# A graph-attention kernel: the adjacency in half-size loads with three buffers, the small buffers over the loaded keys, and an eighth block of each tile transposed by DMA

## The reference

```
h = max(layernorm(x), 0)                       # 8192 x 128
s = leaky_relu(h @ ks.T, slope 0.2)            # 8192 x 8192
s = where(adj > 0, s, -9e15)
attn = softmax(s, axis=1)
out = x + attn @ ks                            # 8192 x 128
```

## Time and profile before

| | |
|---|---|
| median of three runs | 1670.91 us |
| the profiled execution: its own time | 1674.09 us |
| its span, first to last instruction | 1672.3 us |
| mean granted TensorE clock | 0.996 |
| TensorE matmuls busy | 1629.2 us (97%) |
| VectorE busy | 1504.9 us (90%) |
| ScalarE busy | 1436.1 us (86%) |
| GpSimd busy | 1048.3 us (63%) |
| DMA, mean rate | 240 GB/s |
| SyncE's queue, time of its packets | 101.3% of 16 engines' span |

### The profile page before, as it was taken

The page is one execution under the profiler, slowest core; times in us unless marked ns, Lnnn a source line. Parts: engine busy times, 40 slices in busy tenths (PEclk is TensorE's granted clock), DMA queues, the critical chain, the costliest instruction groups (busy, mean ns, idle before and its releaser), DMA issues.

```text
span 1672.3 us, 38378 instructions
## 1 busy us (share of the span) xinstructions
PE 1629.2 (97%) x13698; PEld 1213.1 (73%) x13698; DVE 1504.9 (90%) x2656; ACT 1436.1 (86%) x2145; POOL 1048.3 (63%) x1096
## 2 busy tenths in 40 slices
PE   5699999999999999999999999999999999999999
PEld 3377777777777777777777777777777777777777
DVE  7999989999999999999998989989989998999896
ACT  6688888888888888888888888888888888888887
POOL 1466666666666765765766766666656666666665
PEclk9999999999999999999999999999999999999999
DMA  6699999999999999999999999999999999999996
GB/s 208 179 240 245 252 240 248 249 241 251 236 250 245 240 257 241 247 253 252 237 243 235 258 251 233 248 252 245 243 230 256 243 246 246 242 253 234 248 251 123
DMA packets 536892, 401.00 MB, mean 240 GB/s; under 512 B 479360, under 2 KB 503936, under 8 KB 503936
## 3 DMA queue, kind: packets, MB, share of 16 engines
q1 hardware_dynamic: 536704, 398.54, 101.3%
HBM read 276.82 MB, written 4.19 MB: 168 GB/s over the span
## 4 chain that ended last, share of the span: by engine, by line
PE 79%; DMA 8%; SPq 3%; ACT 2%; DVE 2%; POOL 2%; issue 1%; POOLq 0%; DVEq 0%
PE ps_out L373 22%; PE ps_T L358 12%; PE ps_out L374 11%; PE ps_scores L347 11%; PE ps_scores L349 11%; PE ps_scores L348 11%; DMA turned<-halves 8%; SPq L238 2%; POOL halves L301 1%; ACT scores L449 1%; ACT scores L440 0%; SPq L225 0%; POOL halves L299 0%; DVE probsT_lo L585 0%; DVE mask L558 0%
## 5 line engine op out<-in xcount | busy, mean ns | idle before, releaser
L576 DVE CUSTOM_DVE_ANT_0 scores<-ps_scores,mask,minus_scale 128x1024 f32<-128x1024 f32 x512 | 653.3, 1276 | 1.7 <-PE ps_scores L349 0.6
L301 POOL TENSOR_TENSOR halves<-scores,halves 128x512 f16<-128x512 f32 x448 | 628.8, 1404 | 36.2
L299 POOL CAST halves<-scores 128x512 f16<-128x512 f32 x448 | 317.8, 709 | 528.0 <-ACT scores L449 499.9
L449 ACT ACTIVATE scores<-scores,neg_max 128x1024 f32<-128x1024 f32 x512 | 583.8, 1140 | 0.0
L440 ACT ACTIVATE scores<-scores 128x1024 f32<-128x1024 f32 x512 | 538.7, 1052 | 15.8 <-DVE pair_min L576 12.7
L457 ACT ACTIVATE probsT_hi<-ps_T 128x512 f16<-128x512 f32 x576 | 343.5, 596 | 203.2 <-PE ps_T L358 199.3
L585 DVE TENSOR_TENSOR probsT_lo<-ps_T,probsT_hi 128x512 f16<-128x512 f32 x576 | 395.2, 686 | 133.1 <-ACT probsT_hi L457 131.5
L373 PE MATMUL ps_out<-keys,probsT_hi 128*128 128x256 f16 x2304 | 443.0, 273 | 6.3 <-issue 4.6
L374 PE MATMUL ps_out<-keys,probsT_lo 128*128 128x128 f16 x2304 | 412.0, 219 | 0.0
L347 PE MATMUL ps_scores<-keysT_hi,hT_hi 128*128 128x512 f16 x1024 | 390.1, 381 | 18.7 <-DVE keysT_lo L542 10.7
L349 PE MATMUL ps_scores<-keysT_hi,hT_lo 128*128 128x512 f16 x1024 | 389.3, 380 | 0.0
(11 more groups left out here) (52 smaller groups left out, 771.1 us busy)
## 6 DMA issues: line engine op xcount, KB each, us to landing
adj_in<-in_adj_dram SPq DMA_DIRECT2D x256, 1024.0 KB, 5.9
turned<-halves SPq DMA_TRANSPOSE x448, 6.3
x_in<-in_x_dram SPq DMA_DIRECT2D x64, 64.0 KB, 2.8
keys_in<-in_L_gnn_ks_dram SPq DMA_DIRECT2D x8, 512.0 KB, 7.3
out_dram<-out_tile SPq DMA_DIRECT2D x64, 64.0 KB, 2.2
```

Source lines behind the costliest of these rows:

```text
L301: nc.gpsimd.tensor_tensor(half[:, BLOCK:2 * BLOCK], probs(t, b), half[:, 0:BLOCK], ALU.subtract) \
L449: nc.scalar.activation(s, s, ACT.Exp, bias=neg_max[:, t % 2:t % 2 + 1], scale=-SLOPE, accum_out=pair_sum[:, t % 2, p:p + 1]).then_inc(prob ...
L576: nc.vector.tensor_tensor_reduce(out=score_pair(q, p), in0=ps_scores[:, slots, :].rearrange("p s k -> p (s k)"), in1=mask[:, (p // 2) % 2, ...
```

## The change

- `BY_DMA` takes block 15 as well: eight blocks of each tile are transposed by DMA and eight by TensorE.
- An adjacency load is half as large (1024 columns, 512 KB) and there are twice as many; one stands ahead of each DMA transpose in SyncE's order, at every odd j. The adjacency buffer has three slots of 2048 columns instead of two, each slot with a semaphore for each of its halves. A load waits for the mask three before instead of two before.
- `halves` and `turned` are no longer tensors of their own, but views of the first 20 KB of each partition of `keys_in`. For the first use of each slot GpSimd and SyncE wait until `split_keys_lo` has read the piece of the keys that lies there.
- `make_mask` waits for two semaphores, one for each half.

```
+    ADJ_SLOTS = 3
-    BY_DMA = tuple(b for b in range(BLOCKS) if b % 2 == 1 and b != 15)
+    BY_DMA = tuple(b for b in range(BLOCKS) if b % 2 == 1)
-        adj_in = sbuf("adj_in", [P, 2, LOAD], int32)
+        adj_in = sbuf("adj_in", [P, ADJ_SLOTS, LOAD], int32)
-        halves = sbuf("halves", [P, R_SLOTS, 2 * BLOCK], fp16)
-        turned = sbuf("turned", [P, D_SLOTS, 2 * PER_BLOCK, P], fp16)
-        adj_loaded = [sem(f"adj_loaded{s}") for s in range(2)]
+        adj_loaded = [sem(f"adj_loaded{s}") for s in range(2 * ADJ_SLOTS)]
+        SLOT = 2 * BLOCK
+        room = keys_in[:, :, :].rearrange("p c d -> p (c d)").bitcast(fp16)
+        halves = room[:, 0:R_SLOTS * SLOT].rearrange("p (s k) -> p s k", s=R_SLOTS)
+        turned = room[:, R_SLOTS * SLOT:(R_SLOTS + D_SLOTS) * SLOT] \
+            .rearrange("p (s k c) -> p s k c", s=D_SLOTS, k=2 * PER_BLOCK)
+
+        def keys_under(slot):
+            return (slot * SLOT) // (2 * PER_PAIR * D) + 1
...
-            def load_adj(q, k):
-                if q > 0 or k >= 2:
-                    sp.wait_ge(mask_ready, q * LOADS + k - 1)
-                sp.dma_start(adj_in[:, k % 2, :], adj[rows(q), k * LOAD:(k + 1) * LOAD]) \
-                    .then_inc(adj_loaded[k % 2], 16)
+            def load_adj(q, p):
+                n = q * PAIRS + p
+                if n >= 2 * ADJ_SLOTS:
+                    sp.wait_ge(mask_ready, n // 2 - ADJ_SLOTS + 1)
+                sp.dma_start(adj_in[:, n // 2 % ADJ_SLOTS, n % 2 * PAIR:(n % 2 + 1) * PAIR],
+                             adj[rows(q), p * PAIR:(p + 1) * PAIR]).then_inc(adj_loaded[n % (2 * ADJ_SLOTS)], 16)
...  turn(t, b), the first six
+                else:
+                    sp.wait_ge(keys_lo_ready, keys_under(R_SLOTS + n))
...
-            load_adj(0, 0)
-            load_adj(0, 1)
+            for p in range(4):
+                load_adj(0, p)
...
-                    if j % 4 == 1:
-                        q, k = divmod((i + 1) * LOADS + j // 4 + 2, LOADS)
+                    if j % 2 == 1:
+                        q, p = divmod((i + 1) * PAIRS + j // 2 + 4, PAIRS)
                         if q < TILES:
-                            load_adj(q, k)
+                            load_adj(q, p)
...  split_half(t, b) on GpSimd, the first four
+                else:
+                    pool.wait_ge(keys_lo_ready, keys_under(n))
...
-                dve.wait_ge(adj_loaded[k % 2], (q * (LOADS // 2) + k // 2 + 1) * 16)
+                n = q * LOADS + k
+                dve.wait_ge(adj_loaded[2 * (n % ADJ_SLOTS)], (n // ADJ_SLOTS + 1) * 16)
+                dve.wait_ge(adj_loaded[2 * (n % ADJ_SLOTS) + 1], (n // ADJ_SLOTS + 1) * 16)
```

More of the change, by code:

```diff
@@ L553, in make_mask @@
             def make_mask(q, k):
-                dve.wait_ge(adj_loaded[k % 2], (q * (LOADS // 2) + k // 2 + 1) * 16)
+                n = q * LOADS + k
+                dve.wait_ge(adj_loaded[2 * (n % ADJ_SLOTS)], (n // ADJ_SLOTS + 1) * 16)
+                dve.wait_ge(adj_loaded[2 * (n % ADJ_SLOTS) + 1], (n // ADJ_SLOTS + 1) * 16)
                 if q > 0 or k >= 2:
                     dve.wait_ge(masked_ready, q * PAIRS + 2 * k - 2)
-                nc.vector.tensor_scalar(mask[:, k % 2, :], adj_in[:, k % 2, :], 0, MASKED, ALU.is_le, ALU.mult) \
+                nc.vector.tensor_scalar(mask[:, k % 2, :], adj_in[:, n % ADJ_SLOTS, :], 0, MASKED, ALU.is_le, ALU.mult) \
                     .then_inc(mask_ready, 1)
```

## The result

The changed kernel takes 1658.6 us (median of five runs, 1658.45 to 1658.78), against 1671.16 us for the kernel before in the same comparison: a ratio of 0.992 (0.990 to 0.993). It is 12.6 us faster (0.8%, clear of the interval) where some 30 were forecast. The span of the profiled executions went from 1672.3 to 1656.8 us, 15.5 us less; the profiled execution of before was 3 us slower than its median.

A forecast was written before the change was run, and what follows sets the result against it. TensorE's own instructions were taken to set the 25.11 us pace per tile. 1674.1 - 27 - 4 - 0.3 = 1642.8 us profiled, 1639.6 on the runs' scale; 1641 us was forecast, range 1633 to 1668.

The forecast's parts named there:

- TensorE's gain: TensorE loses one group of transposes per tile: 62 x 0.435 = 27 us saved, period 24.67 us.
- GpSimd's block: GpSimd's 2.11 us more per tile fits its idle 4.49 us before the next tile's block 1; cost 0.
- forecast without excess: Case where all irregular excess goes and VectorE's finish of the tile costs nothing: 1636 us, low end of the forecast.
- in the same place: VectorE loses 0.69 us and ScalarE one instruction per tile, more than TensorE's 0.44, so neither gets nearer to the bound.
- rival (c): TensorE, freed of 0.44 us, waits for another, such as last row parts or exponentials: 1670 us, chance 0.05.
- DMA: DMA engines' work with eight transposes and half-size loads: 23.4 us of a 24.67 us tile, 95% occupied, fits.
- clean price: DMA cost without competing traffic: 1.53 us per transpose, 2.5 us per 1 MB load; 1 us slices gave 21.6 us per tile.
- rival (b): DMA engines become the bound, share over 1 meaning full: slower, +103 to +134 us, up to 1805 us, chance 0.17.
- SyncE's order: In SyncE's queue transposes issue up to 4 us earlier, behind 512 KB; half the 8 us excess, 4 us, saved.
- small things: New waits on the keys at first slot use, bounds 0 to 3 us, and make_mask's second wait; both taken 0.
- the tail: End of the kernel, last output sums after block 15's split: taken -0.3 us, bounds -1.5 and +1.
- rival (a): Turned blocks land late from a DMA queue and TensorE waits, losing half the gain: 1657 us (1650 to 1668), chance 0.15.

The follow-up runs named there:

- e3: The changed kernel, but GpSimd makes block 15's lo part only after VectorE's mask at place 0 of the same step: 1636.9 us, ratio 0.979.
- e4: The changed kernel with VectorE's two operations at place 0 swapped, lo part of block 12 first, then the mask: 1636.95 us, ratio 0.979.
- e8: e4 with block 2 by DMA as well, nine blocks of each tile by DMA: 1614.9 us, ratio 0.966.
- e5: The kernel before, with GpSimd also splitting block 15 into an unread spare buffer, no DMA added: 1694.1 us, ratio 1.013.
- e7: e4 with two spare DMA transposes more per tile, of constant data into an unread buffer: 1725.3 us, ratio 1.031.
- e6: e4 with one spare DMA transpose more per tile, of constant data into an unread buffer: 1637.1 us, ratio 0.979.
- e9: e4 with two adjacency buffers instead of three, loads still half-size: 1636.5 us, ratio 0.978.
- e10: e4 with three buffers but loads of 1 MB at places 1, 5, 9, 13: 1649.2 us, ratio 0.985.

## Why the prediction was wrong

- **TensorE's gain, right.** 0.435 us per tile and 27 us were priced; e3 and e4 run at 24.68 us against 24.67 forecast.
- **GpSimd's block, the step that failed.** The prediction put block 15 into GpSimd's idle 4.49 us "with 2.4 us over" and cost it at 0. The room on GpSimd's own timeline was there. It did not ask which VectorE instruction runs in that gap. It was a mask whose delay has little cover behind it (the later masks that are held up in e8 cost TensorE next to nothing): 0.85 us longer, of which 0.36 reach TensorE, 62 x 0.36 = 22 us. e5 shows exactly this price without the rest of the change, e3 and e4 take it away alone. With it, 1636 us (forecast without excess) becomes 1658, the measured time. A sign of it stood in the rows: the earlier trace rows have GpSimd's lo part at 1.16 us and the earlier trace rows its mean at 1.40, and where it started beside a mask it took 2.02 us before the change too.
- **The statement that VectorE and ScalarE lose more than TensorE "in the same place"** was used against rival (c). VectorE's saved lo part stands at place 3, behind the wait at place 2, so it could not pay for it. Rival (c) was given 5% and had the right victim in kind (another wait takes the saved time), but not the mechanism.
- **DMA, right in outcome, mis-sized.** 23.4 us of work per tile was to fit, and did: one wait of 0.3 us for a turned block is left. The sum was too high: nine transposes fit in 24.24 us (e8) where 24.9 was worked out. Its "23.1 us at the clean price" does not start from the clean sum of 21.0 us but from the 21.6 of the slices (54 of which, not "nearly half", lie under 1). From 21.0, nine make 24.4 us and ten 25.9, close to e8's 24.24 and to e7's mean period of 26.1; which term is off is not shown. Of the ways to read the share, rival (b)'s (over 1 means full) is refuted by e6 at 1.13.
- **SyncE's order, right effect, for half a wrong reason.** All 8 us of excess went, where 4 were counted. The cause given first, the wait for masks with two buffers, is refuted by e9; the one given beside it (512 KB instead of 1 MB ahead of a transpose), with the even order, is what carries it (e9 without the third buffer has no excess, e10 with it has 15 us).
- **The small things and the tail** held: the new waits on the keys show as 6.5 us of SyncE's time, at the first transposes, and the first full tile starts 0.3 us earlier than before (82.26 against 82.57); the tail gave 1.6 us, just past its bound of 1.5.
- **The range held by luck.** 1658.6 us lies between the stated 1633 and 1668, and within the 1650 to 1668 of rival (a). But (a) means turned blocks that come late, and they land after 4.9 us in the median, earlier than before. The mechanism that took 22 us of the gain is in none of the rivals.

Not settled: why the tenth transpose in e7 costs as much as it does. It may be DMA work alone, or the spare transposes' place in SyncE's order, ahead of the next real ones. Which of size and order of the loads ends the excess is open too. What in e8 gives the 3 us of excess was not tried either.

## What to carry to other kernels

When work is moved to an engine with room, look up what the other engines run in that very gap, not only how long the gap is, and look for operations that take longer in some places of the trace than in others: here GpSimd's took 1.16 or 2.02 us, and an idle GpSimd was what kept VectorE's mask fast. If they meet, one wait or one swap of two neighbours can be worth more than the change (22 us against 13). And where small urgent transfers share a queue with large patient ones, halving the large ones and spacing them evenly did what a further buffer did not.

## What the runs showed of the hardware

- VectorE's mask (int32 to bf16, 128 x 2048) and GpSimd's two-input operation hold each other up. The mask takes 1.23 us alone and 2.08 to 2.11 us if it starts 0.16 to 0.13 us after GpSimd's 1.16 us operation. The other way round GpSimd's operation takes 2.02 us, as here in the changed kernel:

```profile
801.20 1.34 DVE L573 TENSOR_SCALAR mask<-adj_in 128x2048 bf16<-128x2048 int32 x1
...
801.54 2.02 POOL L314 TENSOR_TENSOR keys_in<-scores,keys_in 128x512 f16<-128x512 f32 x1
```

- The Trainium skill says so in "SBUF — State Buffer" (Who interferes with whom): the two engines share a pair of ports, and if VectorE's instruction runs in a mode that uses both (a `tensor_scalar` like the mask can), whoever starts first holds the pair for its whole instruction. By that rule the mask would have ended at 808.91 + 1.23 = 810.14 us; it ended at 809.99, so the trace agrees within 0.15 us. The same 0.15 us is missing in each of these meetings: in e5 the mask would end at 827.52 and ends at 827.37, in e4 it would take 1.38 us and takes 1.23, and GpSimd's operation above would end at 803.70 and ends at 803.56. The rule stood against this change and was not weighed.
- Not every pair fits it. GpSimd's one-input operation L300 (128 x 128) starts 0.46 us before a mask, and yet the mask keeps its 1.22 us and GpSimd's takes 1.83 instead of the 0.80 of before. So the recorded start does not always tell which of the two is held up:

```profile
819.61 1.83 POOL L300 TENSOR_SCALAR x_norm<-x_in,mean_var,rstd 128x128 f32<-128x128 f32 x1
...
820.08 1.22 DVE L573 TENSOR_SCALAR mask<-adj_in 128x2048 bf16<-128x2048 int32 x1
```

- The DMA share is no measure of fullness: from 1.07 a ninth transpose per tile was free (e6, 1.13), and at 1.15 the engines kept up in e8 and not in e7. In e6 as in e8 they moved 272 and 273 GB/s, the most of all versions.
